# Recurrent products in two strips of 64 weight columns, in a GRU and in a gated recurrence

## What is computed

```python
x = x + linear_attention(local_attention(x, cond))
x = x + moe(GRU(cond, x))                      # GRU over 256 steps, top-1 of 8 experts
x = x + diff_attention(gated(cond, x))         # gated recurrence over 256 steps
x = x + moe2(modulated(x, cond))               # top-2 of 8 experts
```

```python
# GRU, state h is 8 x 128
r = sigmoid(xr_t + h @ W_hr)
z = sigmoid(xz_t + h @ W_hz)
n = tanh(xn_t + r * (h @ W_hn + b_hn))
h = (1 - z) * n + z * h
# gated recurrence
gate = sigmoid(h @ Wh.T + z_t @ Wz.T + b)
h = tanh(h * (1 - alpha) + gate * z_t)
```

## Time and profile before

| | us |
|---|---|
| median of the runs | 1484.99 |
| lowest and highest run | 1479.08, 1485.76 |
| the profiled execution: its time | 1482.67 |
| its span, first to last instruction | 1479.6 |
| busy in it: PE, PEld, DVE, ACT, POOL | 1376.7, 968.0, 724.5, 674.7, 154.1 |
| mean granted TensorE clock | 0.966 |

### The profile page before, as it was taken

How to read it: one execution, slowest core, us unless ns; L and a number is a source line. 1 busy time by engine, 2 the same in 40 slices (tenths; PEclk the granted TensorE clock), 3 DMA queues, 4 the chain that set the end, 5 groups by cost and what they waited for, 6 DMA issues and landing times. The chain is left out here.

```text
span 1479.6 us, 25632 instructions
## 1 busy us (share of the span) xinstructions
PE 1376.7 (93%) x8736; PEld 968.0 (65%) x8743; DVE 724.5 (49%) x2455; ACT 674.7 (46%) x2433; POOL 154.1 (10%) x253
## 2 busy tenths in 40 slices
PE   8999988999989999999999999899999999839994
PEld 5333332677767999999999997555445444725663
DVE  3577766556453444544544457533333333772223
ACT  3322312556533666666666654244444444623442
POOL 4000003000010000000000000110000000326652
PEclk8999989999999999999999999899999999969997
DMA  5000000000002000000000000100000000001113
GB/s 169 1 0 0 1 0 1 1 1 1 2 23 92 2 2 1 2 1 2 1 2 1 2 1 2 37 22 22 22 23 22 26 4 1 16 15 44 42 42 100
DMA packets 27817, 27.65 MB, mean 19 GB/s; under 512 B 2381, under 2 KB 22346, under 8 KB 27562
## 3 DMA queue, kind: packets, MB, share of 16 engines
q1 hardware_dynamic: 21082, 16.71, 3.8%
q0 software_dynamic: 2496, 5.12, 1.2%
q10 hardware_dynamic: 4112, 4.19, 1.0%
HBM read 21.36 MB, written 4.65 MB: 18 GB/s over the span
## 5 line engine op out<-in xcount | busy, mean ns | idle before, releaser
L1774 PE MATMUL spare<-identb 128*128 128x512 bf16 x760 | 207.7, 381 | 0.0
L1103 ACT ACTIVATE ghid<-gh_ps,cols 128x128 f32<-128x128 f32 x512 | 160.3, 364 | 68.0 <-PE gh_ps L1062 68.0
L1062 PE MATMUL gh_ps<-hist,w 128*128 128x128 f32 x1024 | 161.0, 278 | 3.4 <-ACT ghid L1103 2.6
L1071 PE MATMUL gy_ps<-w2e,ghid 128*128 128x128 f32 x1024 | 156.2, 275 | 0.6 <-DVE g_diff L1158 0.3
L1731 PEld LDWEIGHTS s_pre<-s,wT 128*128 128x128 f32 x512 | 77.9, 190 | 103.4 <-ACT s L1789 101.8
L1062 PEld LDWEIGHTS gh_ps<-hist,w 128*128 128x128 f32 x1024 | 135.9, 189 | 4.8 <-ACT ghid L1103 4.0
L1071 PEld LDWEIGHTS gy_ps<-w2e,ghid 128*128 128x128 f32 x1024 | 135.1, 191 | 1.4 <-issue 0.9
L1249 PE MATMUL pre_z<-hist,gru_w 128*128 128x128 f32 x512 | 121.2, 317 | 0.0
L1836 DVE TENSOR_TENSOR_SCAN targ<-gates,pairs 128x16 f32<-128x16 f32 x256 | 49.2, 192 | 130.6 <-ACT gates L1786 130.6
L1774 PEld LDWEIGHTS spare<-identb 128*128 128x128 bf16 x760 | 78.0, 118 | 43.6 <-issue 3.7
L1731 PE MATMUL s_pre<-s,wT 128*128 128x8 f32 x512 | 98.8, 265 | 4.8 <-ACT s L1789 0.6
(11 more groups left out here) (438 smaller groups left out, 2479.5 us busy)
## 6 DMA issues: line engine op xcount, KB each, us to landing
w<-in_L_ffn_W SPq DMA_DIRECT2D x1, 2048.0 KB, 9.7
raw<-in_L_ffn_wg SPq DMA_DIRECT2D x8, 256.0 KB, 3.0
raw<-in_L_ffn_wu SPq DMA_DIRECT2D x8, 256.0 KB, 2.8
raw<-in_L_ffn_wd SPq DMA_DIRECT2D x8, 256.0 KB, 2.6
wqkv<-in_L_attn_Wqkv SPq DMA_DIRECT2D x1, 1536.0 KB, 6.8
mrow<-mt SPq DMA_DIRECT2D x8, 128.0 KB, 1.8
y_top<-yrow SPq DMA_DIRECT2D x4, 256.0 KB, 5.4
y_next<-yrow ACTq DMA_DIRECT2D x4, 256.0 KB, 6.1
```

Of the source, the lines that this page charges most:

```text
L1062: mm = nc.tensor.matmul(h_bank[w % rings][:, P * f:P * f + P], w1[:, e, c0:c0 + P], tokens(grp), start=True, stop=True)
L1071: mm = nc.tensor.matmul(y_bank[v % rings][:, 0:P], hid[v % 2][:, f, :], w2[:, e, f, :], start=(f == 0), stop=(f == NF - 1))
L1103: nc.scalar.activation(hid[v % 2][:, 2 * half + f, :], h_bank[w % len(h_bank)][:, P * f:P * f + P], ACT.Relu, bias=n.cols[:, at:at + 1]).t ...
L1774: nc.tensor.matmul(spare[:, :], n.identb[:, :], four, start=True, stop=True)
```

## The change

Each recurrent product becomes two: the first has weight columns 0 to 63 and writes partitions 0 to 63 of the same PSUM columns, the second has columns 64 to 127 and writes partitions 64 to 127. Both move the same operand as before. The semaphore is incremented by the second alone. In the GRU this holds for r, n and z. Besides, the first 15 GRU steps have four spare products instead of five, and the x steps of the gated recurrence one wide spare instead of two.

```diff
-    FILL = 5
+    FILL = 4
     BURST = 23
+    STRIP = 64
...
                         for out, i, rhs, ready in ((gate_slot(pre_r, s), 3, now, r_pre), (first(n_slot(s)), 5, now, n_pre), (z_out, 4, ahead, z_pre)):
-                            nc.tensor.matmul(out, n.gru_w[:, i, :], rhs, start=False, stop=True,
-                                             skip_group_check=True).then_inc(ready, 1)
+                            for c in range(0, P, STRIP):
+                                mm = nc.tensor.matmul(out[c:c + STRIP], n.gru_w[:, i, c:c + STRIP], rhs, start=False, stop=True,
+                                                      skip_group_check=True)
+                            mm.then_inc(ready, 1)
...
-            "x": (2, 2), "mod": (2, 0), "w": (1, 2)}
+            "x": (1, 2), "mod": (2, 0), "w": (1, 2)}
+    STRIP = 64
...
-                    nc.tensor.matmul(pre[s // G % 2][:, at:at + B], wT[:, 0, :], s2[:, 8 * s:8 * s + B],
-                                     start=False, stop=True, skip_group_check=True).then_inc(pre_in, 1)
+                    for c in range(0, P, STRIP):
+                        mm = nc.tensor.matmul(pre[s // G % 2][c:c + STRIP, at:at + B], wT[:, 0, c:c + STRIP], s2[:, 8 * s:8 * s + B],
+                                              start=False, stop=True, skip_group_check=True)
+                    mm.then_inc(pre_in, 1)
```

## The result

| | before | changed |
|---|---|---|
| median of the runs (13 each), us | 1484.06 | 1488.67 |
| lowest, highest | 1478.06, 1488.20 | 1486.72, 1494.75 |
| span of the profiled execution | 1479.6 | 1486.0 |
| GRU, first weight load of r in step 0 to the first in step 255 | 429.8 | 443.4 |
| gate recurrence, the same with the loads of s_pre | 307.1 | 300.0 |

The ratio is 1.0047 (95% interval 1.0029 to 1.0065): 4 to 10 us slower. The ratio itself is inside the half per cent that the prediction called no change, and its interval reaches a little beyond. It is made of two parts of opposite sign, as forecast, each larger than their sum: +13.6 us in the GRU and −7.2 us in the gate recurrence. One execution of the kernel before, run beside `gate_only`, took 1713.76 us at a mean granted clock of 0.736; it is left out of the ratios, and so is the profiled execution of `gate_narrow_spares`.

The account below looks back on a forecast made before the run. The prediction took the GRU's bound to pass from the dependent chain to TensorE, as width changes uncover weight loads. GRU +11 us and gate recurrence −8.7 us made +2.3: 1485 us by the profile, 1487 named against the median, range 1470 to 1508.

Parts of the forecast that it names:

- The bound: GRU plain step: the dependent chain ends last, TensorE has almost nothing to spare; after the change TensorE bounds it.
- Strips' latency: Both recurrences: an 8-column product in two strips gives its result 0.10 us sooner after the state.
- GRU plain step: Plain expert steps of the GRU: 1.69 us instead of 1.64, some 182 steps, +10.0 us.
- GRU other steps: 58 GRU steps with logits, transposes, bias or input loads: +0.06 us each as the mean, +3.5 us.
- First 16 steps: Start of the GRU, one spare less: 1.58 us between steps instead of 1.75, −2.6 us.
- Four-spare steps: 164 gate recurrence steps: 1.185 us instead of 1.19, nearly the whole gain lost, −1.3 us.
- The rest of the gate recurrence: 84 qk, job, x, input, w and v steps: −0.095 us each, −8.0 us; 7 bias steps +0.6 us.
- Sum: Whole kernel: GRU +11 us and gate recurrence −8.7 us give +2.3 us.
- A: Both loops: change of width costs nothing, plain GRU steps chain-bound at 1.42 us, about 1417 us in all; chance 0.12.
- B: GRU: z's two strips stream one after the other, +54 us, 1541 us; chance 0.05.
- C: Both loops: strips of one product load in turn, +129 us, 1614 us; chance 0.03.
- D: Either loop: the clock falls in stretches, costing 10 to 30 us, 1497 to 1517 us; chance 0.08.

Follow-up runs that it names:

- gate_only: Against the kernel before: strips in the gate recurrence and one wide spare in its x steps, GRU unchanged; ratio 0.9969.
- gate_narrow_spares: Against the kernel before: recurrent products full, only the gate recurrence's wide spares cut to 64 weight columns; ratio 1.0199.
- gru_all64: Against the kernel before: strips of 64 for all products in the GRU loop except transposes, gate recurrence unchanged; ratio 0.9560, median 1416.72 us.

## Why the prediction was right, point by point

**The bound** was read rightly, and so was what the change does to it. The rule from the earlier trace rows, that a load after a change of width begins 0.07 before the modelled end, held in the plain GRU steps and the four-spare steps of the changed kernel (0.07 to 0.08), and `gate_narrow_spares` shows it without any strips in pairs. There the step got longer though the number of products stayed; in `gru_all64` it got shorter though their number doubled. That run shows the reverse: no change of width, no gap, and the step falls to the chain.

**Strips' latency**: forecast 0.10, measured 0.09 (gates after 0.34; reset 536.65 − 536.31 = 0.34).

**GRU plain step**: forecast 1.69, measured 1.707. The term was +10.0 us and came out at +11.8: 174 steps that went from 1.638 to 1.707, and 8 of the 182 that carry one logits product of a block besides and went from 1.791 to 1.831. What was mis-sized is z's end and what follows it: the prediction had the second pass begin 0.39 after the first load and gh's load at 0.60; the trace has them at 0.40 and 0.61, and from gh's load to gy's modelled end it is 1.17 and not 1.16. The chain behind it is shorter than I thought: forecast 1.42, in gru_all64 1.39. narg follows reset by 0.21 and not 0.29, a figure taken from the earlier trace rows as a handover, while there narg was waiting for n; and tanh follows narg by 0.26 and not 0.22.

**GRU other steps**: +0.06 each, 3.5 us, was too little. Steps with transposes went from 1.897 to 2.034, those with a bias product from 1.679 to 1.764, input steps from 1.776 to 1.859, those with a logits product only from 1.806 to 1.843; in all +4.3 us. **First 16 steps**: 1.58 forecast, 1.580 measured, −2.5 us for the 15; no run tells apart what the spare product less and the strips each did there. GRU in all +11 forecast, +13.6 measured.

**Four-spare steps**: 1.185 forecast, 1.188 measured.

**The rest of the gate recurrence**: −8.0 us forecast. Jobs, x, input and most qk steps fell to 1.10 as said. The step that failed is the one that took the qk step of the earlier trace rows for all 28. Seven of them, one each of w and v with them, do their product late, because PE waits for ACT to copy the previous one. In the changed kernel:

```profile
1003.51 0.20 PEld L1736 LDWEIGHTS s_pre<-s,wT 128*64 128x64 f32 x4 [0.46 <-ACT s L1795]
...
1004.00 0.30 PEld L1760 LDWEIGHTS s_pj<-s,wk 128*128 128x128 f32 x2 [0.29 <-ACT qk L1822]
...
1004.54 0.38 PE L1780 MATMUL spare<-identb 128*128 128x512 bf16 x1
...
1004.85 0.20 PEld L1736 LDWEIGHTS s_pre<-s,wT 128*64 128x64 f32 x4 [0.42 <-ACT s L1795]
```

Here too the load waits for 0.07 before the spare's modelled end (1004.92): the step takes 1.34 instead of 1.19. Before, the load ran under the spare and the late product cost nothing. The qk steps together gained 0.9 us instead of 2.7. The bias steps missed the other way. They were to pay 0.08 to 0.10 each and fell from 1.193 to 1.165: the prediction counted the cover lost at the step's end and not that the bias product, and the spare behind it, start 0.10 earlier, since they stand behind the strips.

Gate recurrence in all −8.7 forecast, −7.2 measured (−8.1 in gate_only). Some 0.85 us of the 7.2 belong to the clock: in the profile before, three steps at the fall of 1119.1 took 1.44, 1.66 and 1.32 instead of 1.19, and the changed kernel's profile has no such fall in its loop after the first 6 us.

**Sum**: +2.3 forecast; the loops give 13.6 − 7.2 = +6.4. The ratio's 4 to 10 us agree with that. Both misses, +2.6 in the GRU and +1.5 in the gate recurrence, make the kernel slower than forecast, and the forecast stays close because both are small. That the median, 1488.67, lies so near to the 1487 named is in part luck: the kernel before came in at 1484.06, 0.9 us under the median that the forecast started from.

**Rivals.** A (free change of width) fell: in every profile read above, the load after a change of width waits as the rule says. B (z's strips in turn) fell: the second strip's pass starts 0.007 after the first's, and z's four matmuls last 0.43 with their modelled tail of 0.165, where in turn the passes alone would take 0.43; eight half-wide gh matmuls last 0.63. C (loads in turn) fell: r's four loads last 0.20 together, a single one 0.13. The rule of the Trainium skill (TensorE: Matmul & The Clock Gate, "Part 3: Packing small matmuls") that was set beside it doesn't fit this trace: it allows a load to overlap matmuls in flight only with another row group, while all these products use all 128 rows and gh's first load in gru_all64 comes while z still streams. D (the clock) didn't happen: 1.00 and 0.99 in the loops, as before. gate_narrow_spares hints that it can, for half-wide products that are not in pairs.

## What to carry to other kernels

A gain in latency that is made by another shape of product must be paid at both borders of that shape: look at what the products before and behind it had been hiding. Here half of the idea cost more than it brought, and the whole of it (the same width for all that stands in the loop) brought 5.7%. And where a step's time is set by two things within 0.1 us of each other, price a representative of each kind of step, the late ones too, since the cover that is lost was covering just those.

## What the runs showed of the hardware that I had not expected

- With spare products on one strip of 64 columns TensorE's clock was at the lower level (0.50) for 30.7, 20.5 and 17.1 us of one profiled execution. In the four profiles with the gate recurrence as before it fell inside the loop for 3.4 to 10.2 us, and in the six with the recurrent product in strips not at all after the first 6 us. What makes the difference is not shown.
- Two strips with 128 moving columns cost almost no more than one full product: 0.63 us for eight, 0.61 for four.
- Strips of 32 in the dense loop left PE idle for "issue" in many pieces of up to 1.2 us, though in the lighter gate recurrence they were the fastest form, 1.08 us a step.
